# LoRA behind three chunks of a tile, its high passes ahead of the low part, and the output copied by two engines

## The reference

```python
def cond(x, language_ids, W, Wr, A, B):      # language_ids: one of 8 per sequence
    base   = einsum('btd,od->bto', x, W)
    logits = einsum('btd,ed->bte', x, Wr) + one_hot(language_ids, 8) * 5.0
    topw, topi = top_k(logits, 2)
    gates  = sum(one_hot(topi, 8) * softmax(topw)[..., None], axis=-2)
    h      = einsum('btd,erd->bter', x, A)   # 8 experts, rank 16: 128 columns
    return base + 2.0 * einsum('bter,bte,eor->bto', h, gates, B)

def ffn(x, sign, scale):
    return einsum('bsi,io->bso', x, sign) * softplus(scale)

out = x + ffn(cond(x, ids, W, Wr, A, B), sign, scale)
```

## Time and profile before

| what | us |
|---|---|
| median of 3 runs | 162.29 (162.12 to 162.74) |
| the profiled execution | 162.27 |
| its span, first to last instruction | 160.4 |
| TensorE busy in the span | 156.9 (98%) |
| VectorE busy | 108.0 (67%) |
| ScalarE busy | 63.8 (40%) |
| GpSimd busy | 51.8 (32%) |
| granted TensorE clock | 1.00 throughout |

### The profile page before, as it was taken

How to read it: one execution, slowest core, us unless ns; L and a number is a source line. 1 busy time by engine, 2 the same in 40 slices (tenths; PEclk the granted TensorE clock), 3 DMA queues, 4 the chain that set the end, 5 groups by cost and what they waited for, 6 DMA issues and landing times.

```text
span 160.4 us, 3654 instructions
## 1 busy us (share of the span) xinstructions
PE 156.9 (98%) x1046; PEld 151.6 (95%) x1046; DVE 108.0 (67%) x451; ACT 63.8 (40%) x178; POOL 51.8 (32%) x50
## 2 busy tenths in 40 slices
PE   8999999999999999999999999999999999999993
PEld 5887899999999999999999999999999999999992
DVE  5899988666656766676666666667666666666651
ACT  3645632244444334334244444433444343334442
POOL 1974535333332313233333333223132333333000
PEclk9999999999999999999999999999999999999999
DMA  5996344324455545444444545545455362222333
GB/s 175 370 161 131 103 129 98 84 71 143 137 140 147 147 142 150 123 135 123 121 124 138 137 139 147 147 143 147 142 148 146 86 186 82 59 70 83 134 130 131
DMA packets 45867, 21.47 MB, mean 134 GB/s; under 512 B 23680, under 2 KB 40864, under 8 KB 45856
## 3 DMA queue, kind: packets, MB, share of 16 engines
q1 hardware_dynamic: 30232, 13.58, 31.0%
q10 hardware_dynamic: 15624, 7.76, 16.8%
HBM read 11.03 MB, written 8.39 MB: 121 GB/s over the span
## 4 chain that ended last, share of the span: by engine, by line
PE 97%; DVE 1%; ACT 1%; issue 0%
PE pair L750 68%; PE pair L786 15%; PE pair L671 3%; PE pair L775 2%; PE pair L691 2%; PE pair L698 2%; PE pair L684 1%; PE pair L731 1%; PE pair L664 1%; PE pair L666 1%; PE pair L665 1%; PE pair L735 1%; DVE ht_lo L580 1%; PE pair L706 0%; PE pair L710 0%; ACT ht_hi L429 0%
## 5 line engine op out<-in xcount | busy, mean ns | idle before, releaser
L327 POOL TENSOR_TENSOR xt_lo<-xt,xt_hi 128x512 fp32r<-128x512 f32 x32 | 41.4, 1293 | 89.8 <-ACT xt_hi L391 86.7
L750 PE MATMUL pair<-wide_hi,xt_lo 128*128 128x392 f32 (+1 forms) x248 | 58.5, 311 | 0.0
L750 PE MATMUL pair<-wide_lo,xt_hi 128*128 128x392 f32 (+1 forms) x248 | 58.4, 312 | 0.0
L750 PE MATMUL pair<-wide_hi,xt_hi 128*128 128x392 f32 (+1 forms) x248 | 58.3, 311 | 0.0
L750 PEld LDWEIGHTS pair<-wide_hi,xt_hi 128*128 128x128 f32 x248 | 38.6, 188 | 0.3 <-issue 0.3
L750 PEld LDWEIGHTS pair<-wide_hi,xt_lo 128*128 128x128 f32 x248 | 38.6, 188 | 0.0
L750 PEld LDWEIGHTS pair<-wide_lo,xt_hi 128*128 128x128 f32 x248 | 38.4, 188 | 0.0
L458 ACT ACTIVATE y<-pair 128x256 f32<-128x256 f32 x31 | 11.9, 385 | 50.9 <-PE pair L786 50.9
L391 ACT ACTIVATE xt_hi<-xt 128x512 fp32r<-128x512 f32 x32 | 20.3, 633 | 7.9 <-DVE xt L499 6.2
L605 DVE TENSOR_TENSOR logits<-pair,bias 128x8 f32<-128x8 f32 x32 | 5.3, 167 | 25.6 <-PE pair L750 25.1
L499 DVE STREAM_TRANSPOSE xt<-x_in 128x512 f32<-128x512 f32 x32 | 22.5, 702 | 0.0
(11 more groups left out here) (105 smaller groups left out, 143.1 us busy)
## 6 DMA issues: line engine op xcount, KB each, us to landing
out<-y SPq DMA_DIRECT2D x31, 256.0 KB, 2.3
x_in<-in_x ACTq DMA_DIRECT2D x104, 64.0 KB, 2.2
h_moved<-h_gated SPq DMA_DIRECT2D x116, 16.0 KB, 1.8
x_in<-in_x SPq DMA_DIRECT2D x24, 64.0 KB, 2.1
w_in<-in_L_cond_W SPq DMA_DIRECT2D x4, 256.0 KB, 4.5
sign_in<-in_L_ffn_sign ACTq DMA_DIRECT2D x3, 256.0 KB, 4.4
sign_in<-in_L_ffn_sign SPq DMA_DIRECT2D x1, 256.0 KB, 5.6
a_in<-in_L_cond_A SPq DMA_DIRECT2D x4, 64.0 KB, 3.9
```

Of the source, the lines that this page charges most:

```text
L327: nc.gpsimd.tensor_tensor(xt_lo[n][:, :, :].rearrange("p j (g b) -> p g j b", g=NQ), xt[n][:, :, :, :], xt_hi[n][:, :, :].bitcast(FP32).re ...
L750: last = nc.tensor.matmul(pair[n][bank][:, at0:at0 + hi - lo], l[:, k, :], w[:, k, lo:hi], start=(opens and k == 0 and l is xt_hi[n] and w ...
```

## The change

TensorE does chunks 0, 1 and 2 of a tile ahead of the LoRA, and chunk 3 behind it. The LoRA waits for `ht_hi` ahead of its first pass and for `ht_lo` only ahead of its third. VectorE copies the first half of y at the end of its step (new instruction), ScalarE the second half alone; TensorE waits for `y_first_copied` at its step's first matmul, and for `y_copied` at the second. From tile 27 on ScalarE copies both halves as before, up to tile 30. In the tail the LoRA of tile 27 stands behind two chunks of bank 0 of tile 30 and no longer behind three, and all LoRAs take the split wait. The store of y waits for both copies.

```diff
-            def store(q, r, d):
+            def store(q, r, d, s):
                 sp_eng.wait_ge(y_copied, RING * q + r + d + 1)
+                if s is None or s + d < LATE - 2:
+                    sp_eng.wait_ge(y_first_copied, RING * q + r + d + 1)
...
-                    if s != TILES - 1 + LAG:
+                    if s is not None and TILES - 2 <= s < TILES - 1 + LAG:
                         nc.scalar.activation(y[n][:, 0:Y0], pair[n][0][:, HEAD:HEAD + Y0], ACT.Copy)\
-                            .then_inc(y_first_copied, 1)
+                            .then_inc(late_first_copied, 1)
...
+                if s is None or LAG <= s < TILES - 2:
+                    o = slot(r, -LAG)
+                    dve.wait_ge(y_summed, done - LAG + 1)
+                    if s is None or s - LAG >= RING:
+                        dve.wait_ge(y_stored[o], 16 * turn(q, r, -LAG))
+                    nc.vector.tensor_copy(y[o][:, 0:Y0], pair[o][0][:, HEAD:HEAD + Y0]).then_inc(y_first_copied, 1)
...
+                            if second_after is not None and k == 0 and bank == 1 and w is wide_hi and l is xt_hi[n]:
+                                pe.wait_ge(y_copied, second_after)
...
+                pe.wait_ge(ht_hi_made, high_then_low)
                 for l, w, stop in ((h_hi, b2_hi, False), (h_hi, b2_lo, False), (h_lo, b2_hi, True)):
+                    if l is h_lo:
+                        pe.wait_ge(ht_lo_made, high_then_low)
...
-                        pe.wait_ge(y_copied, done - RING + 1)
+                        pe.wait_ge(y_first_copied, done - RING + 1)
...
-                    wide(r, range(KC // 2), BANKS, opens=True, low_after_high=(s == 1))
+                    wide(r, range(KC - 1), BANKS, opens=True, low_after_high=(s == 1),
+                         second_after=(done - RING + 1 if s is None or s >= RING else None))
...
-                    wide(r, range(KC // 2, KC), BANKS, signals=True)
+                    wide(r, [KC - 1], BANKS, signals=True)
...
                 pe.wait_ge(y_first_copied, s - RING)
-                wide(before, range(KC - 1), (BANKS[0],), opens=True)
-                pe.wait_ge(ht_lo_made, s - 3)
-                lora((s - 4) % RING, (0, 1)).then_inc(y_summed, 1)
-                wide(before, [KC - 1], (BANKS[0],)).then_inc(head_ready, 1)
+                wide(before, first, (BANKS[0],), opens=True)
+                lora((s - 4) % RING, (0, 1), s - 3).then_inc(y_summed, 1)
+                wide(before, second, (BANKS[0],)).then_inc(head_ready, 1)
...
-                pe.wait_ge(y_first_copied, s - RING + 1)
+                pe.wait_ge(late_first_copied, 1)
```

More of the change, by code:

```diff
@@ L200, in adaln_ffn_kernel @@
         y_first_copied = sem("y_first_copied")
+        late_first_copied = sem("late_first_copied")
         last_summed = sem("last_summed")
@@ L286, in turnover @@
                 if s is None or s >= LAG + LEAD:
-                    store(q, r, -LAG - LEAD)
+                    store(q, r, -LAG - LEAD, s)
             for s in range(LAG + LEAD):
@@ L737, in _, with wide @@
             last.then_inc(b2_summed, 1)
-            def wide(r, chunks, cols, opens=False, signals=False, low_after_high=False):
+            def wide(r, chunks, cols, opens=False, signals=False, low_after_high=False, second_after=None):
                 n = slot(r)
@@ L779, in first_tile, with lora @@
                                 last.then_inc((head_ready, wide_done)[bank], 1)
-            def lora(n, banks, h_hi=ht_hi, h_lo=ht_lo):
+            def lora(n, banks, high_then_low, h_hi=ht_hi, h_lo=ht_lo):
+                pe.wait_ge(ht_hi_made, high_then_low)
                 for l, w, stop in ((h_hi, b2_hi, False), (h_hi, b2_lo, False), (h_lo, b2_hi, True)):
+                    if l is h_lo:
+                        pe.wait_ge(ht_lo_made, high_then_low)
                     for bank in banks:
@@ L805, in step @@
                     if s is None or s >= RING:
-                        pe.wait_ge(y_copied, done - RING + 1)
+                        pe.wait_ge(y_first_copied, done - RING + 1)
                     if s == RING - 1:
                         pe.wait_ge(b2_lo_made, 1)
-                    wide(r, range(KC // 2), BANKS, opens=True, low_after_high=(s == 1))
+                    wide(r, range(KC - 1), BANKS, opens=True, low_after_high=(s == 1),
+                         second_after=(done - RING + 1 if s is None or s >= RING else None))
                 if has(s, -LAG):
-                    pe.wait_ge(ht_lo_made, done - LAG + 1)
-                    lora(slot(r, -LAG), (0, 1)).then_inc(y_summed, 1)
+                    lora(slot(r, -LAG), (0, 1), done - LAG + 1).then_inc(y_summed, 1)
                 if s != 0 and has(s, 0):
-                    wide(r, range(KC // 2, KC), BANKS, signals=True)
+                    wide(r, [KC - 1], BANKS, signals=True)
             def finish(s):
@@ L846, in finish @@
                 turn_h(s)
-                pe.wait_ge(ht_lo_made, s)
-                lora(before, (0, 1)).then_inc(y_summed, 1)
+                lora(before, (0, 1), s).then_inc(y_summed, 1)
                 wide(r, second[:1], (BANKS[1],))
-                pe.wait_ge(ht_lo_made, s + 1)
-                lora(r, (0,), ht_hi_last, ht_lo_last).then_inc(last_summed, 1)
+                lora(r, (0,), s + 1, ht_hi_last, ht_lo_last).then_inc(last_summed, 1)
                 wide(r, second[1:], (BANKS[1],))
-                lora(r, (1,), ht_hi_last, ht_lo_last).then_inc(y_summed, 1)
+                lora(r, (1,), s + 1, ht_hi_last, ht_lo_last).then_inc(y_summed, 1)
             pe.wait_ge(ident_made, 1)
```

6 lines of the change are left out of this document (2 added, 4 removed).

## The result

| | before | after |
|---|---|---|
| median, us | 162.44 (162.12 to 163.37) | 163.93 (163.34 to 164.21) |
| ratio to before, 95% interval | | 1.0076 (1.0051 to 1.0102) |
| the profiled execution | 162.27 | 163.85 |
| its span | 160.4 | 162.0 |
| TensorE busy | 156.9 | 158.2 |

I had forecast 161.9 and a range up to 163.3. The median lies above both. The granted clock is 1.00 in both, so TensorE did not run slower; it waited more. A part of this waiting stands in its busy time, which rose by 1.3: two matmuls behind a late weight load are recorded as 0.54 long and not as 0.46.

A forecast was written before the change was run, and what follows sets the result against it. It took TensorE, busy 98% of the span, as the bound, so only its waits matter: 162.27 - 0.63 (LoRA stalls) + 0.25 (register instructions) - 0.02 (tail) = 161.87, so 161.9 us, range 161.2 to 163.3.

The forecast's parts named there:

- The stalls of the LoRAs: Steps 3 to 29: four LoRAs lengthened by waiting for ht_lo beside xt_lo; all four stalls go, -0.63 us.
- Part 2: Loop steps: how late GpSimd and VectorE become, timed from a step's first matmul; VectorE's copy runs 3.73 to 4.15.
- lateness e: Step boundary: a TensorE step starting e late costs e/2 per step over some 26 steps, or 13e.
- the last link of Part 2: Step boundary: weight load follows VectorE's copy by 0.06, at 4.21 against 4.18 undisturbed, so 0.03 late.
- The first 0.03 to 0.07 are free: Late weight loads on TensorE: a load costs less than its lateness, the first 0.03 to 0.07 us nothing.
- nominally the copy costs TensorE nothing: Step boundary: VectorE's new copy adds 0 us to TensorE's steps, with no slack left.
- The register waits: First step of each hardware-loop turn: its wait on a separate register instruction costs e of 0.05, +0.25 us in all.
- DMA issues of ScalarE stand ahead of its copy as before and end before 3.61: ScalarE's queue in each step: its DMA issues do not delay its copy of y, due at 3.61; no cost.
- The copy comes late in every step: Rival, wait for y_first_copied at a step's first matmul: slower, 162.7 for e = 0.08 up to 163.7; chance 0.22.
- The other two rivals: Loop: copy fits and xt_lo does not hold ht_lo, 161.2, chance 0.16; stalls return at the boundary, 162.2, chance 0.12.
- The rule on consecutive VectorE instructions: VectorE's copy starts 0.08 before h_gated ends, leaving 161.9; without the exception for ops not held, 162.9.
- The rule on the lock: ht_lo beside xt_lo: ends 0.25 after GpSimd, as the row shows; a fully blocking lock would give 163.7.

The follow-up runs named there:

- e12: The kernel after with the two waits ahead of a step's first matmul swapped, y_first_copied asked for first; 163.02 us, ratio 1.0041 to before.
- e1: The kernel after with TensorE's wait for xt_lo of the next tile moved ahead of the last chunk of the tile before; 162.33 us, ratio 0.9981 to before.
- e11: e8 with tile 27's LoRA back behind three chunks of bank 0 in the tail; 161.20 us, ratio 0.9920 to before.
- e8: The kernel after with xt_lo's wait moved a chunk earlier, xt_hi ahead of ScalarE's copy, two of four load issues behind it; 161.13 us, ratio 0.9907 to before.
- e10: e8 with the wait for xt_lo put back beside y_first_copied at the step's first matmul; 161.13 us, ratio 0.9907 to before.
- e6: The kernel after with the LoRA back behind two chunks in the steps; 161.99 us, ratio 0.9970 to before.
- e7: The kernel before with only the split wait: ht_hi ahead of the LoRA's first pass, ht_lo ahead of its third; 161.80 us, ratio 0.9954 to before.
- e9: The kernel after with a third, long-satisfied wait (b2_lo_made) at a step's first matmul; 162.86 us, ratio 1.0036 to before.
- e5: The kernel after with only one of the four x load issues per tile from tile 4 on; 162.81 us, ratio 1.0019 to before.

## Why the prediction was wrong

**What held.** The stalls of the LoRAs were 0.63, had the cause I gave, and went. Of Part 2 every link on ScalarE, GpSimd and VectorE is right: `xt_lo` until 1.57, `ht_lo` until 1.82, `h_gated` 3.46 to 3.81, copy 3.73 to 4.14 (forecast 3.73 to 4.15). It was also right that a boundary with lateness e costs e at every second step only, but for the 0.04 in the first step of each turn: the measured +1.24 over 26 steps is 0.095 for each of 13 pairs of steps. The tail came within 0.02.

**The step that failed: the last link of Part 2.** "From the end of a VectorE instruction to the weight load that waited for it was 0.06", I took from the LoRA of step 8. That load had one wait. The load at the boundary has two, I even named both, and by the records shown with e12 the late one stands on an instruction of its own ahead of the load: 0.115. e1, with nothing changed but the place of the other wait, has 0.053, near what I had taken. With the due place at 4.16 (the loads ahead end at 38.23, 4.16 into step 4), the load is 0.10 late and not 0.03.

**The sentence beside it failed too.** "The first 0.03 to 0.07 are free" came from one LoRA (0.32 late, 0.25 lost). Here a load 0.10 late cost 0.09; in e1 loads 0.02 to 0.04 late cost 0.01 to 0.02. The first matmul behind a late load starts 0.03 after it (38.33 to 38.36) and not 0.12, which looks like a gift; but it then takes 0.54 for two and not 0.46, and the time is gone one matmul later. So the term "nominally the copy costs TensorE nothing" was mis-sized: it measured 0.08 to 0.09 for a pair of steps, some 0.9 us over the eleven pairs without a long step, and with the register waits 1.24, where I had 0.25 for both.

**The register waits** were there and cost some 0.08 in each of the four turns, 0.3 in all, near my 0.25: in steps 8, 12, 16 and 20 the copy ends at 4.23 and not 4.15, since ScalarE's copy starts some 0.13 later in the step before.

**"DMA issues of ScalarE stand ahead of its copy as before and end before 3.61"** failed in two steps and cost 0.89. The trace of before had the warning: at this very place three issues took 1.83 and, on SyncE's queue, four took 3.38. I had read ScalarE's issues in one step only. What was neither forecast nor a rival is that the issues themselves were longer in after (3.10 against 1.83 in step 25). Whether the change made them longer or chance did is not shown: e11, with the LoRA behind three chunks too, has none over 0.8.

**Missed on the other side**: with the LoRA behind three chunks an undisturbed step takes 4.283 us and not 4.300, -0.43. e8, e10 and e11 show 4.28, e6 and e7, with it behind two chunks, 4.300; so it is the order of TensorE's work. Why is open.

**The rivals.** "The copy comes late in every step" had the place, the sign and the arithmetic right (13e, 162.7 for e = 0.08), but not the cause: it was to need a copy that ends later than 4.15, and outside the loop's register waits the copy ended at 4.14 to 4.15. What came late was the load behind it. I gave this rival 0.22, since "each link was taken from a row". The links on the other engines deserved that trust; the link to TensorE was the row of a different form, and I gave it no bound from above. A copy with zero slack should have had more. The other two rivals did not come about: GpSimd's `xt_lo` does hold `ht_lo`, and the stalls came back as 1.24 and not as 0.6.

**The rule on consecutive VectorE instructions.** The copy starts at 37.80, 0.08 before `h_gated` ends at 37.88. That is the exception which the Trainium skill, VectorE: DVE Perf Modes, section "The DRAIN you can't avoid", makes for ops that are not held, and this case's trace agrees with it.

**The rule on the lock.** `ht_lo` ends 0.25 after `xt_lo` (35.89 and 35.64), less than its own 0.39, in every step of after where they meet. An exclusive lock that "fully blocks", as in the Trainium skill, SBUF — State Buffer, section "SBUF: two separate sides", would leave all 0.39 for the time behind GpSimd; the measurement decides against it here as well, in all 27 places where the two meet (0.24 to 0.26) and not in one.

## What to carry to other kernels

Where a new wait will be the last to be met at a boundary without slack, look at what instruction it stands on: a wait on the weight load itself let it start 0.05 us behind the releaser, one on an instruction ahead of it 0.07 to 0.13. In e1 the other wait, met earlier, was asked for a chunk sooner, and no cost of that can be seen. An edit that moves work from one side of a buffer's reuse to the other needs the slack on both sides, counted with the longest DMA issue that the trace shows on the engines involved, not with a typical one. Try the smallest part of a change alone: the split wait, some five lines of e7, gave back nearly all that the LoRAs had lost, and the parts that stood beside it lost more than that.

## What the runs showed of the hardware

- **A wait's place.** The same semaphore, the same producer and the same load: 0.053 us with the wait on the load, 0.115 on a semaphore instruction of 0.051 ahead of it, 0.123 to 0.133 on a register instruction of 0.032 to 0.042 ahead of it, 0.070 on a semaphore instruction that holds a second, earlier-met wait as well (e9).
- **Long DMA issues at fixed places.** An issue of ScalarE's that usually takes 0.3 to 0.6 us takes 1.4 to 1.8 in steps 5, 9 and 25 of after, and SyncE's moves of h are long at the same times (3.30 for four in step 25, 3.17 in step 9, against 2.49). Ten of the fourteen kernels have one to three of over 1 us on ScalarE's queue, always in these steps and nearly the same by number (the 26th, 42nd and 106th, or one or two behind); before, e5, e7 and e11 have none. Fewer issues per step (e5) gave none, and with two of them behind the copy one of 1.39 (e8) and one of 1.63 (e10) cost nothing; what makes them long is open.
- **Order of matmuls.** 26 steps of the same 30 matmuls take 4.300 us each with six LoRA matmuls in the middle and 4.283 with the six ahead of the last chunk. I have no row that says why.
